# Message additions back on the vector engine, in a new order of a build block on three engines

## The reference, cut to what matters

```
Wh = h @ W + b
dot, nr, nc = Wh[row] . Wh[col], |Wh[row]|, |Wh[col]|
sim = dot / max(nr * nc, 1e-8)
base = adj * softplus(...) * (row != col)
prop_pos = segment_sum(base * relu(sim) * Wh[col], row)
prop_neg = segment_sum(-base * relu(-sim) * Wh[col], row)
x = x + scale * (c0 * prop_pos + c1 * prop_neg + c2 * Wh)
```

## Time and profile before

| | us |
|---|---|
| runs, median (lowest to highest) | 1067.99 (1063.03 to 1068.55) |
| profiled execution, its own time | 1059.61 |
| its span | 1057.9 |
| PE, DVE, ACT busy over the span | 840.5, 854.9, 619.2 |
| POOL busy over the span | 175.8 |
| the build's blocks 1 to 24 and the last messages | about 148 to 702 |

### The profile page before, as it was taken

One profiled execution on the slowest core, in us unless ns is written; L12 is line 12 of the kernel. 1 busy time (PEld: TensorE's weight loads), 2 busy tenths in 40 slices (PEclk: granted clock), 3 DMA queues, 4 the chain that ended last, 5 costly groups with the idle time before them and its releaser, 6 DMA issues. The chain is left out here.

```text
span 1057.9 us, 33568 instructions
## 1 busy us (share of the span) xinstructions
PE 840.5 (79%) x14240; PEld 593.2 (56%) x14240; DVE 854.9 (81%) x1214; ACT 619.2 (59%) x2090; POOL 175.8 (17%) x364
## 2 busy tenths in 40 slices
PE   0695558878787878878778787744999998999997
PEld 0362435544445545455444554424999998996653
DVE  8986778878888888888888888656666798587896
ACT  0764447767767777677776767617999942112000
POOL 4815711112111121111211112100000000000000
PEclk9987569999999999999999999976999999998999
DMA  9933116566666667666675666759700000783893
GB/s 210 232 115 86 54 41 155 136 151 161 153 139 147 147 165 160 139 147 150 165 157 135 150 144 161 164 159 391 302 2 2 2 2 1 307 310 130 323 388 128
DMA packets 44697, 164.32 MB, mean 155 GB/s; under 512 B 14245, under 2 KB 16375, under 8 KB 40823
## 3 DMA queue, kind: packets, MB, share of 16 engines
q1 hardware_dynamic: 33990, 133.22, 42.6%
q0 software_dynamic: 8288, 27.59, 12.8%
q10 hardware_dynamic: 2256, 1.23, 0.5%
HBM read 78.63 MB, written 63.72 MB: 135 GB/s over the span
## 5 line engine op out<-in xcount | busy, mean ns | idle before, releaser
L1170 PE MATMUL b_ps<-b_mv,b_soh 64*128 64x50 bf16 (+1 forms) x9600 | 192.3, 189 | 119.9 <-DVE b_mv L1055 66.4
L1170 PEld LDWEIGHTS b_ps<-b_mv,b_soh 64*128 64x128 bf16 x9600 | 164.2, 95 | 171.9 <-DVE b_mv L1055 110.9
L1390 PE MATMUL layers_ps<-layers_u,layers_c 128*128 128x192 bf16 x2500 | 210.9, 247 | 11.4 <-ACT layers_u L1572 8.8
L1390 PEld LDWEIGHTS layers_ps<-layers_u,layers_c 128*128 128x128 bf16 x2500 | 208.0, 98 | 16.5 <-DVE layers_y L1696 8.0
L946 ACT ACTIVATE b_c_row<-b_ps 128x300 bf16<-128x300 f32 (+1 forms) x275 | 119.7, 435 | 79.5 <-PE b_ps L1170 72.6
L1093 DVE TENSOR_TENSOR b_y<-b_sim,b_ps 128x512 f32<-128x512 f32 (+1 forms) x175 | 109.9, 628 | 63.9 <-PE b_ps L1224 59.3
L964 ACT ACTIVATE b_pos<-b_ps,k_coef 128x1024 f32<-128x1024 f32 x100 | 92.8, 928 | 91.9 <-PE b_ps L1170 90.7
L1055 DVE TENSOR_TENSOR b_mv<-b_mv,b_parts 128x2808 bf16<-128x2808 bf16 x100 | 145.6, 1456 | 0.0
L1581 ACT ACTIVATE k_passed<-layers_c 128x128 bf16<-128x128 bf16 x450 | 131.4, 294 | 0.0
L1051 DVE TENSOR_TENSOR b_soh<-k_numbers,b_bits 128x2304 bf16<-128x2304 bf16 x100 | 121.9, 1219 | 0.0
L1082 DVE SCALAR_TENSOR_TENSOR b_sim<-b_ps,k_coef,b_pos 128x1024 f32<-128x1024 f32 x100 | 104.6, 1046 | 16.6 <-ACT b_pos L964 16.6
(11 more groups left out here) (275 smaller groups left out, 1123.4 us busy)
## 6 DMA issues: line engine op xcount, KB each, us to landing
layers_c<-g_blocks SPq DMA_DIRECT2D x25, 1600.0 KB, 9.2
g_blocks<-b_g_row SPq DMA_DIRECT2D x52, 400.0 KB
c_blocks<-b_c_row SPq DMA_DIRECT2D x25, 800.0 KB
g_blocks<-head_odd SPq DMA_DIRECT2D x48, 400.0 KB
layers_c<-c_blocks SPq DMA_DIRECT2D x12, 1600.0 KB, 26.3
k_passed<-b_sent POOLq DMA_DIRECT2D x24, 768.0 KB, 6.5
prep_attr<-in_edge_attr SPq DMA_DIRECT2D x2, 1883.0 KB
prep_attr<-in_edge_attr SPq DMA_DIRECT2D x1, 1876.0 KB
```

Of the source, the lines that this page charges most:

```text
L1170: return nc.tensor.matmul(out, lhsT, rhs, start=start, stop=True, skip_group_check=True)
L1390: return nc.tensor.matmul(out_, lhsT, rhs, start=start, stop=True, skip_group_check=True)
```

## The change

`send`, `message`, the tile `sent` and the semaphore `summed` go. DVE makes the four additions of every block, each straight from the PSUM bank. The order tables of PE and DVE are new, ACT has a table of its own, and `hot` is split, so that `soh` and `mv` stand apart. SP writes the gates earlier (behind lots 2 and 6 instead of 4 and 8).

```
-BYSUM = NB - 1
...
-LEAVE = [("lot", 4), ("lot", 8), ("prop", 5), ("prop", 6)]
+ORDER = [("sims", 0), ("lot", 0), ("lot", 1), ("turn", 0), ("lot", 2), ("sims", 1), ("turn", 1), ("lot", 3), ("lot", 4),
+         ("turn", 2), ("lot", 5), ("sims", 2), ("turn", 3), ("prop", 0), ("prop", 1), ("lot", 6), ("turn", 4), ("lot", 7),
+         ("sims", 3), ("lot", 8), ("turn", 5), ("prop", 2), ("prop", 3), ("turn", 6), ("lot", 9), ("lot", 10), ("prop", 4),
...
+AORDER = [("sims", 0), ("lot", 0), ("lot", 1), ("lot", 2), ("sims", 1), ("lot", 3), ("lot", 4), ("sims", 2), ("lot", 5),
...
-        sent = [l.sb(f"sent{i}", [P, 3 * 512 + P]) for i in range(1)]
...
-            def message(v):
-                pool.wait_ge(s["added"], NG * v + NG + 1)
...
-                if isinstance(w, int):
-                    message(b - 1)
...
-                    sp.wait_ge(s["evac"], 3 * NL * b + 6 + 3 * 4)
+                    sp.wait_ge(s["evac"], 3 * NL * b + 6 + 3 * 2)
                     gated_out(b - 1, 0, 2)
-                    sp.wait_ge(s["evac"], 3 * NL * b + 6 + 3 * 8)
+                    sp.wait_ge(s["evac"], 3 * NL * b + 6 + 3 * 6)
                     gated_out(b - 1, 2, 4)
...
-            def send(v, g):
...
-                for what, i in ORDER:
+                for what, i in AORDER:
                     if what == "lot":
                         evacuate(r, w, par, i)
...
-                if isinstance(v, int) and v < BYSUM:
-                    return
                 dve.wait_ge(s["propped"], NC * v + (2 * NC + 1 + min(2 * g + 2, NC)))
-                if isinstance(v, int) and v == BYSUM and g == 0:
-                    dve.wait_ge(s["summed"], 32 * BYSUM)
                 part, bank = k["passed"][0:m, g, 0:n], PR if g < NG - 1 else AT
                 nc.vector.tensor_tensor(part, part, ps[0:m, bank, 0:n], ALU.add).then_inc(s["added"], 1)
```

More of the change, by code:

```diff
@@ L671, in _ @@
                 sp.wait_ge(s_kept, 80)
[L674 to L676 removed]
+ORDER = [("sims", 0), ("lot", 0), ("lot", 1), ("turn", 0), ("lot", 2), ("sims", 1), ("turn", 1), ("lot", 3), ("lot", 4),
+         ("turn", 2), ("lot", 5), ("sims", 2), ("turn", 3), ("prop", 0), ("prop", 1), ("lot", 6), ("turn", 4), ("lot", 7),
+         ("sims", 3), ("lot", 8), ("turn", 5), ("prop", 2), ("prop", 3), ("turn", 6), ("lot", 9), ("lot", 10), ("prop", 4),
          ("prop", 5), ("prop", 6)]
[L678 to L683 removed]
+VORDER = [("soh", 1), ("sim", 0), ("y", 0), ("hi", 1), ("mv", 1), ("hi", 2), ("y", 1), ("sim", 1), ("soh", 2), ("y", 2),
+          ("mv", 2), ("y", 3), ("hi", 3), ("sim", 2), ("y", 4), ("add", 0), ("soh", 3), ("sim", 3), ("mv", 3), ("y", 5),
+          ("add", 1), ("soh", 0), ("y", 6), ("hi", 0), ("mv", 0), ("add", 2), ("add", 3)]
+AORDER = [("sims", 0), ("lot", 0), ("lot", 1), ("lot", 2), ("sims", 1), ("lot", 3), ("lot", 4), ("sims", 2), ("lot", 5),
+          ("lot", 6), ("sims", 3), ("lot", 7), ("lot", 8), ("lot", 9), ("lot", 10)]
 def rounds_of(eng, table):
@@ L709, in build @@
         begun = l.sb("begun", [P, 6])
-        sent = [l.sb(f"sent{i}", [P, 3 * 512 + P]) for i in range(1)]
-        sim, scale = [l.sb(f"sim{i}", [P, 1024]) for i in range(2)], sent[0][:, 0:512]
+        sim, scale = [l.sb(f"sim{i}", [P, 1024]) for i in range(2)], l.sb("scale", [P, 512])
         y = [l.sb(f"y{i}", [P, 1024]) for i in range(2)]
@@ L720, in build @@
         s = {n: l.sem(n) for n in names.split()}
-        s_win, s["further"], s["summed"] = k["win"], k["further"], k["summed"]
+        s_win, s["further"] = k["win"], k["further"]
         s_stored = [l.sem(f"stored{i}") for i in range(2)]
@@ L992, in step @@
                         positive(w - 1, i)
[L993 to L996, removed]
             def end(r):
@@ L1120, in first @@
                 for o in range(4):
-                    onehots(r, r * NB, o, "hi")
-                    onehots(r, r * NB, o, "hot")
+                    for part in ("hi", "soh", "mv"):
+                        onehots(r, r * NB, o, part)
                     if not again(r) and o == 2:
@@ L1127, in first @@
                     count_degrees()
-                onehots(r, r * NB + 1, 0, "hi")
-                onehots(r, r * NB + 1, 0, "hot")
+                for part in ("hi", "soh", "mv"):
+                    onehots(r, r * NB + 1, 0, part)
                 if not again(r):
@@ L1138, in step @@
                 for what, i in VORDER:
-                    if what in ("hi", "hot"):
+                    if what in ("hi", "soh", "mv"):
                         if i:
@@ L1913, in four_layers @@
         k["rows"], k["win"] = [top.sem(f"rows{g}") for g in range(len(GATES))], [top.sem(f"win{g}") for g in range(len(GROUPS))]
-        k["further"], k["starts"], k["summed"] = top.sem("further"), top.sem("starts"), top.sem("summed")
+        k["further"], k["starts"] = top.sem("further"), top.sem("starts")
         table = top.sb("table", [1, 2], I32)
```

7 lines of the change are left out of this document (5 added, 2 removed).

## The result

The changed kernel takes 1038.86 us, the median of four runs (1036.95 to 1039.57), against 1065.51 us (1061.11 to 1068.55) of the kernel before beside it: the ratio is 0.975, with a 95% interval of 0.971 to 0.979. The forecast was 1054, with a range of 1043 to 1065.

What follows compares the result with a forecast made beforehand. The build was taken to go at the pace of DVE's work plus three waits for PE. Gains of 9.4 us (24 blocks x 0.39), 2.6 at the end and 2.3 from long blocks, 14.3 together, took 1068.0 to 1054 us, range 1043 to 1065.

Steps and rivals of the forecast that it cites:

- a game of turns of DVE and PE: Build: y frees the bank, PE transposes, the next y waits; three DVE waits of 1.23, 0.90 and 0.40 us a block.
- DVE's sum, 21.5 us: DVE's work in a block: 19.48 us in the new order plus 2.0 us of additions, against a pace of 21.96 us.
- the pairs: DVE instructions directly behind the one they wait for: sim before y 1.38 us, hi before mv 0.44 us.
- The waits vanish: DVE's three waits a block go, as PE is ready 0.6 us or more before DVE at y; gain 0.5 us a block.
- The first rival: The game of turns stays: DVE keeps 2.5 us of waits, 24.0 us a block, 1114 us in all; chance 9%.
- POOL holds the next soh up by 0.1 us: POOL's copies, run beside two additions after mv 0, delay DVE's next soh by about 0.1 us; bounds 0 and 0.46.
- the walk: Step-by-step timing from the end of y 5: POOL's weights' copies come about 0.2 us behind the start of mv 0.
- Half of the long blocks, 2.3 us: Of 4.6 us that single blocks lose on PE, half counted as covered, 2.3 us; bounds 0 and 4.6.
- The end, 2.6 us: Behind block 24, the wait for the last transfer goes: 2.2 us at y 3 plus 0.4 for transposes.
- the forecast's 0.4 for slow transposes: Behind block 24, transposes took 1.07 instead of 0.66 us behind PE's long idle time; 0.4 us to be gained.
- From profile to median: The 14.3 us gain was taken from the median of before, 1068.0 us, 8.4 us above its profiled 1059.6, giving 1054.

Runs made afterwards that it cites:

- experiment 2: The kernel before with only the new order, additions still by transfer: 1015.53 us; the changed kernel with the old three orders, additions on DVE: 1070.66 us.
- experiment 5: The changed kernel with three more POOL copies of 128x128 float32 per block, released by chunk 4's prop: 1043.7 us, ratio 0.980.
- Experiment 1: The kernel before with its adding transfers replaced by a tiny POOL instruction: 1061.62 us; the changed kernel with two unread adding transfers per block: 1040.3 us.
- experiment 6: The kernel before, unchanged, profiled a second time: 1056.23 us, against a median of 1060.82 us on its chip.

## Why the prediction was wrong in size and right in kind

- *What bounds before: a game of turns of DVE and PE.* Right. The waits went where the order gave each of them a wide tile, and experiment 2 shows that they are the gain: 50 us by the order alone.
- *DVE's sum, 21.5 us.* Right within 0.12: measured 21.37, with the additions at 0.60 and the pairs 0.01 to 0.02 us below the forecast. That the block *is* this sum is shown by 22.10 with 0.73 us more, and by 20.76 with the pairs apart.
- *The waits vanish.* Right: no idle row in the steady blocks, PE waits for DVE five times a block. The first rival (24 us a block) failed; where only DVE's order is new its mechanism is seen, 1.90 us in front of one y.
- *POOL holds the next soh up by 0.1 us.* Mis-sized: the two meet where the walk put them, and DVE loses nothing. The Trainium skill, "SBUF — State Buffer", section "Who interferes with whom", says that whoever issues first keeps the other out. The trace agrees with DVE first (POOL's copy 1.51 us long). What the prediction priced was POOL's last copy still running when the next soh is due: by the rows it does run 0.13 us into soh, in experiment 5 even 1.50 us, and soh starts on time in both. With the 0.1 us that DVE's sum lies lower, a block gains 0.59 instead of 0.39 us: 13.0 us over 22 blocks, where 9.4 were forecast over 24.
- *Half of the long blocks, 2.3 us.* Mis-sized: all 4.6 are gone. Experiment 1 shows that the transfers do not make these blocks long; about 1.4 us of the 4.6 are one stretch of low clock, and 1.9 us are four stalls of PE. In the changed kernel no stall of 0.3 us stands in the build, and in its twin with later gate writes two of 0.32 us lengthen no block. The stalls end at a fixed distance behind packets of the instruction queue; that these packets are their cause is argued, not tried.
- *The end, 2.6 us.* Right: 2.3 by experiment 1, which takes only the transfers away. Of this the forecast's 0.4 for slow transposes did not go as reasoned: the low clock is in the last interval without the transfers too, and in that of the profile after. The last two intervals and the tail of the changed kernel gain 3.4, pace included.
- *From profile to median.* The step that failed most. The prediction laid its 14.3 us on the median of before, 8.4 us above its profile, as if this distance belonged to any version. It does not: the profile of before lies 5.9 us under the median of the four runs beside after (one more run took 2.5 of the 8.4 us away), that of after stands 0.7 above its median. This is 9.1 of the 15 us by which the forecast was off. The cause stays open. The longer executions of before are those with a lower granted clock; that the evenly filled build keeps the changed kernel out of it is argued from the stretches counted in the steady blocks (one against none), and was not tried. That before's profile is not one of its runs is the other reading (experiment 6).

Against before's profile 14.3 us were forecast and 20.1 measured: 3.6 more from the pace, 2.3 from the long blocks, 0.8 from the end, 1.3 less from the start, and the rest of 0.4.

## What to carry to other kernels

A change in two parts may be a gain and a loss: run each half, above all one that moves work onto the engine that is to become the bound, here worth 50 us and -23 us. When one engine is full, a step is its own sum, so put an independent instruction between each pair of which the second waits for the first (0.11 to 0.16 us each, 15 us here for three moves in a table). And do not carry a kernel's distance between profile and median over to the next version: here it was 5.9 us in one and 0.7 us, the other way, in the other.

## What the runs showed of the chip that was not expected

- *Extra work on the bounding engine can cost twice.* 0.73 us more DVE work a block brought the low clock into 13 of 22 blocks, 0.5 to 0.66 us each time, and 1.27 us more into every block, 1.25 us each. In the blocks of 22.10 us PE is busy for 17.52 us, as in the changed kernel's of 21.37, so its idle time grew by what was added. The Trainium skill, "TensorE: Matmul & The Clock Gate", section "HAM oscillation — how this bites in real kernels", describes kernels in which PE's pauses between bursts of matmuls lower the clock again and again. Its first example pauses for transfers; here the pauses are waits for DVE, and the granted clock of 0.80 in the stretch shown agrees.
- *PE can stall for 0.3 to 1.7 us in a run of small products or at its end with nothing to wait for* (once 2.2 us in front of a sims), at about the same places of the program in the kernel before with and without its transfers, and more often where a block is shorter (12 times in the order with transfers). Each of the 52 stalls counted ends 1.2 to 1.6 us after a 16 KB packet of the instruction queue.
- *POOL's copies stretch beside DVE's one-hot instructions and DVE's don't:* 0.23 us for 64 columns beside an addition, 1.51 for 128 beside mv, 1.64 beside soh. The 0.46 us that DVE lost at 111 us were not seen in the steady blocks.
